# Attention: one denominator matmul per half on sums made partly by chained DMA additions, values from step 2, the reciprocal in a ring bank

## What is computed

```python
x_ln = layer_norm(x_flat, g1, beta1)                      # 16 images, 1024 positions, 64 channels
q, k, v = jnp.split(x_ln @ w_qkv.T, 3, axis=-1)           # 8 heads of 32
scores = jnp.einsum('bhqd,bhkd->bhqk', q, k) * HEAD_DIM ** (-0.5)
attn = jax.nn.softmax(scores, axis=-1)
out = jnp.einsum('bhqk,bhkd->bhqd', attn, v)
```

## Time and profile before

| | us |
|---|---|
| median of 3 runs | 3538.03 (3535.53 to 3543.32) |
| profiled execution | 3552.51 |
| its span in the trace | 3550.8 |
| attention phase in it, about | 62 to 1860 |
| one group there (two halves), about | 54.0 |

### The profile page before, as it was taken

One profiled execution on the slowest core, in us unless ns is written; L12 is line 12 of the kernel. 1 busy time (PEld: TensorE's weight loads), 2 busy tenths in 40 slices (PEclk: granted clock), 3 DMA queues, 4 the chain that ended last, 5 costly groups with the idle time before them and its releaser, 6 DMA issues. The chain is left out here.

```text
span 3550.8 us, 55181 instructions
## 1 busy us (share of the span) xinstructions
PE 3105.6 (87%) x18038; PEld 1163.9 (33%) x18038; DVE 2563.1 (72%) x3346; ACT 2048.7 (58%) x2445; POOL 2264.7 (64%) x748
## 2 busy tenths in 40 slices
PE   6999999999999999999986999556788878878887
PEld 2333333333333333333322333422223223222222
DVE  5788888888778888888831222245888888888888
ACT  3577777777667777777752333225545555555554
POOL 0688888888878888888871000015766666576665
PEclk7899999999999999999998999777999999999989
DMA  3122222222222222222224110133443434344343
GB/s 106 37 55 55 52 55 63 52 55 49 61 49 55 55 46 63 52 55 62 47 50 124 75 73 12 56 121 120 144 153 115 155 123 150 122 146 159 109 155 118
DMA packets 83956, 301.94 MB, mean 85 GB/s; under 512 B 14112, under 2 KB 15204, under 8 KB 75444
## 3 DMA queue, kind: packets, MB, share of 16 engines
q1 hardware_dynamic: 69460, 215.06, 17.9%
q0 software_dynamic: 14272, 83.94, 10.7%
HBM read 192.42 MB, written 39.39 MB: 65 GB/s over the span
## 5 line engine op out<-in xcount | busy, mean ns | idle before, releaser
L550 DVE TENSOR_REDUCE at_pmax<-at_ring 128x1 f32<-128x512 f32 x2048 | 1299.6, 685 | 299.8 <-PE at_ring L340 294.7
L610 POOL TENSOR_TENSOR at_prob_sums<-at_prob_sums,at_probs 128x2048 f32<-128x2048 f32 x256 | 1159.8, 4530 | 209.3 <-ACT at_probs L512 198.5
L512 ACT ACTIVATE at_probs<-at_sc 128x1024 f32<-128x1024 f32 x1024 | 992.9, 1021 | 382.2 <-PE at_sc L411 378.9
L1664 POOL TENSOR_TENSOR ss_drive<-ss_du,ss_bsb 128x1024 f32<-128x1024 f32 x261 | 611.2, 2353 | 270.1 <-DVE ss_state L1621 262.6
L404 PE MATMUL at_sc<-at_QT,at_KT 32*128 32x512 f32 x4096 | 739.1, 630 | 6.7 <-issue 5.9
L1564 ACT ACTIVATE ss_decay<-ss_delta,ss_a 128x512 f32<-128x512 f32 x520 | 354.5, 687 | 446.8 <-DVE ss_state L1617 300.7
L423 PE MATMUL at_O<-at_probs,at_V 128*32 128x512 f32 x4096 | 521.0, 603 | 26.1 <-DVE at_att L571 25.8
L1453 PE MATMUL ss_Y<-ss_seen,ss_ident 128*128 128x512 f32 x1032 | 523.3, 631 | 0.0
L340 PE MATMUL at_ring<-at_KH,at_QH 32*128 32x512 bf16 x2048 | 430.1, 389 | 6.3 <-DVE at_pmax L550 3.0
L1629 DVE TENSOR_TENSOR ss_seen<-ss_state,ss_C 128x1024 f32<-128x1024 f32 x259 | 316.3, 1221 | 87.6 <-PE ss_C L1441 79.8
L1621 DVE TENSOR_TENSOR_SCAN ss_state<-ss_decay,ss_state,ss_drive 128x512 f32<-128x512 f32 x259 | 332.2, 1283 | 31.4
(11 more groups left out here) (196 smaller groups left out, 2795.4 us busy)
## 6 DMA issues: line engine op xcount, KB each, us to landing
ss_bsb<-scratch_rows SPq DMA_DIRECT2D x265, 512.0 KB, 6.8
at_probs<-at_probs POOLq DMA_DIRECT2D x64, 1024.0 KB, 6.9
scratch_attn<-at_att SPq DMA_DIRECT2D x64, 256.0 KB, 2.0
fc_att<-scratch_attn SPq DMA_DIRECT2D x32, 512.0 KB, 5.8
ss_xn<-scratch_xm SPq DMA_DIRECT2D x34, 256.0 KB, 5.5
at_xn<-scratch_xn SPq DMA_DIRECT2D x32, 256.0 KB, 3.8
ss_xw<-scratch_xw SPq DMA_DIRECT2D x17, 256.0 KB, 3.8
ln_x<-in_x SPq DMA_DIRECT2D x8, 512.0 KB, 4.5
```

Of the source, the lines that this page charges most:

```text
L512: nc.scalar.activation(probs[:, kb, two, :].rearrange("p h q -> p (h q)"), sc[:, two, :].rearrange("p h q -> p (h q)"), ACT.Exp, scale=SCA ...
L550: nc.vector.tensor_reduce(pmax[:, quad // 2, h, quad % 2:quad % 2 + 1], ring[:, unit[3], :], AX_X, ALU.max, negate=True).then_inc(max_done, 1)
L610: nc.gpsimd.tensor_tensor(prob_sums[:, half, :, :], before, probs[:, k, :, :], ALU.add).then_inc(pool_sums, 1)
L1664: nc.gpsimd.tensor_tensor(drive[:, n % DEPTH, :], du[:, par, :], bsb[:, n % SLOTS, :], ALU.mult).then_inc(drive_done, 1)
```

## The change

One denominator block is left in a half. GpSimd adds blocks 2, 4, 6, 7 to block 0 with four vector additions. SP copies block 1 of `probs` into a new buffer `odd_sums` (`copy_block`), two DMAs from GpSimd's queue add blocks 3 and 5 to it, one after the other, and a third adds `odd_sums` to `prob_sums`. The denominator becomes a unit of the ring, `den`, in s14 (of the group's first half) and s6 (of the half before): at the end of that step, after `values`. ScalarE's Ln and Exp read and write this ring bank, after the exponentials of s6 or s14. VectorE's product is done at the start of s7 or s15, ahead of that step's reductions, and frees the bank (`od_free`). `O` is free after `take_v`, so `values` begin at kb 2 with two blocks, and there is one block in each of the other steps but kb 1.

```diff
-    POOL_ADDS = (1, 2, 4, 6, 7)
-    ONTO, ADDED, ADDED_BEFORE = 3, 5, 6
+    POOL_ADDS = (2, 4, 6, 7)
+    COPIED, DMA_ADDS = 1, (3, 5)
-    extra = {0: [("q", 0)], 1: [("k", 0)], 3: [("k", 1)], 7: [("turn", 1)], 9: [("q", 1)], 15: [("turn", 0)]}
+    extra = {0: [("q", 0)], 1: [("k", 0)], 3: [("k", 1)], 6: [("den", 1)], 7: [("turn", 1)], 9: [("q", 1)], 14: [("den", 0)],
+             15: [("turn", 0)]}
-    V_AT, SUMS_AT = 1, 2
+    V_AT = 1
-    PV_AT = {0: (LAST_KB,), 3: (0,), 4: (1, 2), 5: (3, 4), 6: (5,), 7: (6,)}
+    PV_AT = {0: (LAST_KB,), 2: (0, 1), 3: (2,), 4: (3,), 5: (4,), 6: (5,), 7: (6,)}
...
+            def copy_block(b, g, half):
+                j = 2 * (GROUPS * b + g) + half
+                if not (isinstance(b, int) and b == 0 and g == 0):
+                    sp.wait_ge(sum_added, DMA * (j - 1))
+                sp.wait_ge(exp_done, 2 * (KB * j + COPIED) + 2)
+                sp.dma_start(odd_sums[:, half, :, :], probs[:, COPIED, :, :]).then_inc(copied, DMA)
+
             def image(b, stage):
+                copy_block(b, 0, 0)
                 if stage != "first":
                     store(b - 1, 1, 1)
+                copy_block(b, 0, 1)
...
                     load_x(b + 1)
                 store(b, 0, 0)
+                copy_block(b, 1, 0)
                 store(b, 0, 1)
+                copy_block(b, 1, 1)
                 store(b, 1, 0)
...
-                    pe.wait_ge(max_done if before[2][1] == "max" else extra_done, unit_count(*before))
+                    if before[2][1] == "den":
+                        pe.wait_ge(od_free, 2 * (before[1] - before[2][2]) + before[2][2] + 1)
+                    else:
+                        pe.wait_ge(max_done if before[2][1] == "max" else extra_done, unit_count(*before))
...
+            def denominator(slot, of_half, half):
+                pe.wait_ge(sum_added, DMA * (of_half + 1))
                 for h in range(GH):
+                    m = nc.tensor.matmul(ring[head(h), slot, :], ones[:, head(h)], prob_sums[:, half, h, :], start=True, stop=True)
+                m.then_inc(extra_ready, 1)
...
             def values(stage, grp, par, half, kb):
                 if kb == 0:
-                    if stage == "first" and half == 0:
+                    if stage == "last":
+                        pe.wait_ge(raw_done, 2 * grp + half)
+                    else:
                         pe.wait_ge(v_done, v_halves(grp, half))
-                    else:
-                        pe.wait_ge(od_free, 2 * grp + half)
...
+            def reciprocal(slot, count, of_half):
+                act.wait_ge(extra_ready, count)
+                nc.scalar.activation(lden[:], ring[:, slot, :], ACT.Ln).then_inc(lden_done, 1)
                 act.wait_ge(lden_done, of_half + 1)
+                nc.scalar.activation(ring[:, slot, :], lden[:], ACT.Exp, scale=-1.0).then_inc(extra_done, 1)
...
+            def normalise(stage, grp, half):
+                if not executed(stage, "den", half, 0):
+                    return
+                unit = unit_of(stage, "den", half)
+                dve.wait_ge(raw_done, 2 * (grp - half) + half + 1)
+                dve.wait_ge(extra_done, unit_count(stage, grp, unit))
+                nc.vector.tensor_tensor(att[:, half, :], att[:, half, :], ring[:, unit[3], :], ALU.mult).then_inc(od_free, 1)
...
                 for s in range(STEPS):
+                    if s % KB == KB - 1 and stage != "lead":
+                        normalise(stage, grp, 1 - s // KB)
...
         def _(pool):
+            def add_odd(grp, half, n):
+                j = 2 * grp + half
+                pool.wait_ge(exp_done, 2 * (KB * j + DMA_ADDS[n]) + 2)
+                if n == 0:
+                    pool.wait_ge(copied, DMA * (j + 1))
+                else:
+                    pool.wait_ge(block_added, DMA * (len(DMA_ADDS) * j + n))
+                pool.sem_inc(add_ready, 1)
+                pool.dma_start(odd_sums[:, half, :, :], probs[:, DMA_ADDS[n], :, :], accum_op=ALU.add).then_inc(block_added, DMA)
...
+            def add_sums(grp, half):
+                j = 2 * grp + half
+                pool.wait_ge(pool_sums, SUMMED * (j + 1))
+                pool.wait_ge(block_added, DMA * len(DMA_ADDS) * (j + 1))
+                pool.sem_inc(sum_ready, 1)
+                pool.dma_start(prob_sums[:, half, :, :], odd_sums[:, half, :, :], accum_op=ALU.add).then_inc(sum_added, DMA)
+
             def period(grp, par, stage):
                 for half in range(2):
+                    add_even(grp, half, 0)
+                    add_odd(grp, half, 0)
+                    add_even(grp, half, 1)
+                    add_odd(grp, half, 1)
+                    add_even(grp, half, 2)
+                    add_even(grp, half, 3)
+                    add_sums(grp, half)
```

More of the change, by code:

```diff
@@ L175, in executed @@
             return ahead
-        return not ahead if stage == "last" else True
+        if stage == "last":
+            return not ahead
+        return not (stage == "first" and kind == "den" and which == 1)
     def period_units(stage):
@@ L380, in turn, with denominators @@
                 m.then_inc(extra_ready, 1)
-            def denominator(src, start, stop):
-                for h in range(GH):
[L384 to L389, removed]
-                else:
[L391 to L397, removed]
+            def denominators(stage, grp, half):
+                if not executed(stage, "den", half, 0):
+                    return
+                unit = unit_of(stage, "den", half)
+                wait_for_bank(stage, grp, unit)
+                denominator(unit[3], 2 * (grp - half) + half, half)
+            def denominator(slot, of_half, half):
+                pe.wait_ge(sum_added, DMA * (of_half + 1))
+                for h in range(GH):
+                    m = nc.tensor.matmul(ring[head(h), slot, :], ones[:, head(h)], prob_sums[:, half, h, :], start=True, stop=True)
+                m.then_inc(extra_ready, 1)
             def scores(stage, grp, par, s):
@@ L439, in period @@
                         values_projected(stage, grp, par, half)
-                    if closes and kb == SUMS_AT:
-                        denominators_added(2 * grp + half - 1, None if stage == "last" else v_halves(grp, half))
-                        denominators_sums(2 * grp + half - 1, was_half)
                     for kind, which in extra.get(s, []):
-                        if kind != "turn":
+                        if kind in MADE_AHEAD:
                             project(stage, grp, par, kind, which)
@@ L454, in period @@
                             turn(stage, grp, which)
+                        if kind == "den" and stage != "lead":
+                            denominators(stage, grp, which)
                     maxima(stage, grp, par, s, (2, 3))
@@ L518, in period @@
                         take_v(grp, par, half)
-                    if closes and kb == SUMS_AT:
-                        reciprocal(2 * grp + half - 1)
                     for kind, which in extra.get(s, []):
@@ L526, in period @@
                             take(stage, grp, unit, nrow[:, which, :])
+                        elif kind == "den":
+                            reciprocal(unit[3], unit_count(stage, grp, unit), 2 * (grp - which) + which)
                         else:
@@ L530, in period @@
                     take_raw(grp, 1)
-                    reciprocal(2 * NG - 1)
+                    reciprocal(0, counted_before(N_EXTRA, grp) + N_EXTRA["last"] + 1, 2 * NG - 1)
             period(-1, 1, "lead")
@@ L588, in period @@
                 if stage == "last":
-                    normalise(grp, 1)
+                    dve.wait_ge(raw_done, 2 * NG)
+                    dve.wait_ge(extra_done, counted_before(N_EXTRA, grp) + N_EXTRA["last"] + 1)
+                    nc.vector.tensor_tensor(att[:, 1, :], att[:, 1, :], ring[:, 0, :], ALU.mult).then_inc(od_free, 1)
             period(-1, 1, "lead")
@@ L596, in period @@
             def period(grp, par, stage):
                 for half in range(2):
-                    for n, k in enumerate(POOL_ADDS):
-                        if k == ADDED_BEFORE:
-                            pool.wait_ge(exp_done, 2 * (STEPS * grp + KB * half + ADDED) + 2)
-                            pool.wait_ge(pv_done, STEPS * grp + KB * half + ONTO + 1)
-                            if not (isinstance(grp, int) and grp == 0 and half == 0):
-                                pool.wait_ge(block_added, DMA * (2 * grp + half))
-                            pool.sem_inc(add_ready, 1)
-                            pool.dma_start(probs[:, ONTO, :, :], probs[:, ADDED, :, :], accum_op=ALU.add).then_inc(block_added, DMA)
-                        pool.wait_ge(exp_done, 2 * (STEPS * grp + KB * half + k) + 2)
-                        if n:
-                            pool.wait_ge(pool_sums, SUMMED * (2 * grp + half) + n)
```

(3 more changed lines are left out.)

53 lines of the change are left out of this document (26 added, 27 removed).

## The result

The changed kernel takes 3557.11 us (median of 4 runs, 3555.16 to 3564.69) where the kernel before took 3539.53 beside it: ratio 1.0054, 95% interval 1.0035 to 1.0073. It is slower by 17.6 us; 3561 was predicted. The profiled execution took 3555.16.

The account below looks back on a forecast made before the run. TensorE was taken as the bound, with late exponentials and the ring and `O` as further limits. 17.6 + 6.9 - 1 = +23.5 us on the profiled 3552.5 gave 3576, or 3561 for the runs; range 3505 to 3605.

Parts of the forecast that it names:

- part 1: TensorE's steps with one denominator block less: s11 2.50, s12 3.15, s13 2.50, s14 4.00; s3 3.82, s4 2.50, s5 3.15, s6 3.35.
- The rule of the late scores: First block starts 1.50 after the step's start or 1.32 after the last step's exponentials, whichever is later; short steps cost 0.65.
- part 2: In s7 and s15 TensorE waits for VectorE's product to free the denominator's bank: values at 2.75, each step 4.34.
- The sum: +0.57 a group over 31 groups, +17.6 us; with +6.9 and about -1 at the end, +23.5 us.
- Paid back twice: The missing block's gain is lost to short steps running into exponentials and to the product holding up every half.
- Rival (a): The bank doesn't stop TensorE, or less: 78 less than forecast, 3483; 3522 if half the wait is lost; chance 0.20.
- part 3: GpSimd and DMAs: less work for GpSimd, last addition issued 4.8 after s8, landing 6.9 later, 9 us to spare.
- Nobody waits: No engine waits for GpSimd's sums or the DMAs in the middle; the new waits were taken as nothing.
- copy 7: The copy of block 1 by SP was taken as 7 us, within bounds of 5.8 and 13.6, at no cost.
- the rest fits ahead of kb 6: kb 5's addition waits 6.9 for kb 3's; the kb 4 vector addition covers 4.5, the remainder fits before kb 6.
- rival (b): DMAs late, TensorE waits for sum_added in s6 and s14: 1 us late gives 3625, 2 us 3689; chance 0.08.
- part 4: End of the attention phase: another DMA of 6.9 before the last denominator matmul, +6.9 once; last group about -1.

Follow-up runs that it names:

- half_exp_before: The kernel before the change, with ScalarE's exponentials computed for only the first head of each pair: 3484.31 us, ratio 0.9845 to the kernel before.
- ln_frees_vector_busy: Changed kernel with Ln freeing the bank, the product on GpSimd, and VectorE doing an unused reduction in the product's place: 3517.84 us, ratio 0.9936 to the kernel before.
- ln_frees_gpsimd: Changed kernel with ScalarE's Ln freeing the bank, Exp writing to SBUF, and the product done by GpSimd a half later: 3503.42 us, ratio 0.9894 to the kernel before.
- copy_twice: Changed kernel with SP first copying each block once more to an unread buffer and waiting for it: 3652.17 us, ratio 1.0310 to the kernel before.
- no_dma_sums: Changed kernel without the copy, the three DMA additions and ScalarE's waits for them: 3546.59 us, ratio 1.0021 to the kernel before.
- ln_frees_gpsimd_end: ln_frees_gpsimd with the last half's last DMA addition replaced by two denominator sets on TensorE: 3491.40 us, ratio 0.9861 to the kernel before.

## Why the prediction held, and where it did not

- **The steps (part 1).** Right to 0.02 in s11 to s14, and in the first half too (s3 3.82, s4 2.49, s5 3.16, s6 3.36 in TensorE's timeline). The rule of the late scores holds.
- **The bank's wait (part 2).** Right: product at 1.63 (1.62), values at 2.76 (2.75). The only term that was off: s15 took 4.24, not 4.34. But measured to the first block of the next step, as the halves are, the two stretches grew by 0.40 and 0.20 (s3 to s8 and s11 to the next s0), where +0.39 and +0.18 were said.
- **The sum.** +0.57 a group was said, +0.49 measured; the steps that I took for unchanged gave 0.11 back (s9 took 0.12 less). Over the middle it is +14.1 (29 groups) and not 17.6 (31 groups). Two terms were not in the sum at all: the first copy of `O` 3.1 earlier, and the group at the loop's turn, 3.1 shorter. Their cause is open, and chance of the single executions is not ruled out.
- **"Paid back twice".** The claim was half wrong. The short steps do run into the exponentials, but half_exp_before shows that the kernel before paid that as well. The prediction's own step times already held both sides (s7 and s15 of before have the late scores, 2.15); only the sentence counted them to the change alone. The bank's wait, and in it VectorE's order, is the loss: 39.3 us come back when the bank is free sooner, 53.7 when VectorE has no product to do either.
- **Rival (a)**, no stop at the bank, priced at 78 below the forecast, needs a bank that is free by 1.19 after the start of s7; in the kernel as it stands the product starts at 1.63, as the prediction held against this rival, and it does not decide. ln_frees_vector_busy and ln_frees_gpsimd are that rival built, and gave 39.3 and 53.7 of the 78.
- **The DMAs (part 3).** "Nobody waits" was right, the working was not. The last addition was issued 11.7 us after the s0 at 920.48 and 7.5 after the s8 at 948.56, not 4.8 (the expectation of copy_twice has the two the other way round). GpSimd's timeline, the issue at 932.14 by itself, and all DMA issues (KB, median us to landing):

```profile
913.18 0.86 POOL L619 DMA_DIRECT2D at_odd_sums<-at_probs  x1 [4.90 <-ACT at_probs L525]
...
921.45 0.87 POOL L619 DMA_DIRECT2D at_odd_sums<-at_probs  x1 [2.84 <-DMA at_odd_sums<-at_probs]
922.05 9.43 POOL L627 TENSOR_TENSOR at_prob_sums<-at_prob_sums,at_probs 128x2048 f32<-128x2048 f32 x2
932.14 0.86 POOL L634 DMA_DIRECT2D at_prob_sums<-at_odd_sums  x1 [0.65 <-POOL at_prob_sums L627]
...
at_prob_sums<-at_odd_sums POOLq DMA_DIRECT2D x1, 1024.0 KB, 7.0
...
at_odd_sums<-at_probs POOLq DMA_DIRECT2D x128, 1024.0 KB, 7.5
at_odd_sums<-at_probs SPq DMA_DIRECT2D x64, 1024.0 KB, 5.3
at_prob_sums<-at_odd_sums POOLq DMA_DIRECT2D x64, 1024.0 KB, 9.6
```

  GpSimd's queue stood until 913.18 for the copy, which SP had issued at 900.41, together with the image load and behind the last addition of the half before: some 12 us, where other copies take 5.3. The row's bracket names ScalarE, whose exponentials of that block had long been done. Then it stood 2.84 for the addition of kb 3, 921.45 - 913.18 = 8.27, not 6.9. The two steps that failed are "copy 7" for the one that meets other transfers, and "the rest fits ahead of kb 6". The Trainium skill ("DMA: Bandwidth & Descriptors", section SWDGE vs HWDGE vs iDMA) says that the transfers of GpSimd and SP go into different queues of the same DMA engines, and that an engine takes turns between its queues. From this the prediction had both transfers up to 5 later, as an estimate, and the trace agrees: 12.2 for the copy where 7 was taken, and 9.9 for the last addition beside it, issued at 899.77, where the one issued at 932.14 took 7.0. That one landed at 939.2, due in s6 at 943.36: 4.2 to spare of the 9. Over all halves but the last and the one at the loop's turn, the trace has 4.7 to spare in the median and 1.0 at least. copy_twice shows that rival (b) was near: some 8 us more, and it decides.
- **The end (part 4).** +8.6, not 6.9. GpSimd issued the last addition at 1864.29, and 7.0 later the denominator went, as said; but 0.6 lies ahead of the issue, and the additions of kb 6 and 7 began 0.8 later against the last copy of `O` (1854.24 to 1857.16; before, 1846.08 to 1849.76), since GpSimd's queue again stood 2.84 for kb 3's addition, and took 0.3 longer. no_dma_sums and ln_frees_gpsimd_end both give it back.

In all: 14.1 + 8.6 - 0.5 - 3.1 - 3.1 = +16.0 in the attention phase of the profiled executions, +17.6 in the runs. Against this +16.0 the sum of +23.5 was too long by its middle (3.5) and by the two terms of -3.1, and too short by 1.7 at the end and 0.5 in the last group. The runs alone don't tell the two sums apart: their interval goes from 12 to 26 us. The mechanism is what the traces bear out.

## What to carry to other kernels

Where a result is written into a ring of buffers, ask who frees that place and what this engine has to do first; a matmul set that was saved gained nothing here, because its buffer was freed by an engine with other work ahead of it, and a copy out that freed it one operation earlier turned a loss of 17.6 us into a gain. Before a loss is put down to a limit that is seen in the changed kernel, price the same limit in the kernel before. And a chain of transfers is costed with the transfers that run beside it, here 12 us and not 5 for a copy, and once more at the end of the phase, where nothing covers it.

## What the runs showed of the hardware

- VectorE's product with both operands in SBUF took 681 to 5689 ns, 3839 in the median, beside GpSimd's additions; with one operand in PSUM 0.68 us. The run was 309 us above the changed kernel; its expectation had the wait, at 133 us at most. A reduction of one SBUF operand, in the same place, took 675 to 687 ns in all 63 halves (ln_frees_vector_busy).
- In copy_twice waits cost TensorE more than their length: with 62 us of waits the phase was 94 longer, and the granted clock was 0.50 to 0.66 in the 3.45 us behind 14 of the 15 waits over 2 us.
- The changed kernel also had such a stretch without a long wait: in the last group the granted clock was 0.57 from 1807.7 to 1814.7, behind waits of 0.78 and 0.21 for VectorE's maxima. no_dma_sums has the same two waits there and no such stretch, and that half takes 25.32 and not 28.62. What parts the two is open.
